# Routed tokens fetched by a slot-to-token table, and router products moved between the first up products

## The chip, the cores and the metric

The kernel runs on one core of a Trainium2 chip. The metric is the device time of one execution in microseconds (us).

## What is computed

Four stages follow each other on the residual `x` of 4 x 512 tokens by 512. The change lies in the second, a mixture of experts:

```python
sh_mid = gelu(einsum('th,ehd->ted', xt, Wsh_up), approximate=False)   # 2 shared experts, width 256
shared_out = einsum('ted,edh->th', sh_mid, Wsh_down)
probs = softmax(xt @ W_router, axis=-1)                               # 16 routed experts
top_v, top_i = top_k(probs, 2)
rt_mid = gelu(einsum('th,ehd->ted', xt, Wrt_up), approximate=False)
routed_out = einsum('ted,edh->th', rt_mid * gate[:, :, None], Wrt_down)
x = x + shared_out + routed_out                                       # xt: x after a layer norm
```

## The kernel before, in words

Each stage is a function with one instruction stream per engine, written out by hand; counting semaphores order the engines. Products are made in fp32r from three passes (`three_pass`, L47): high by high, high by low and low by high parts, where ScalarE makes the high part with a copy and VectorE the low part with a subtraction. `batch_product_phase` comes first, then `experts_phase` (L563), whose two parts the change touches, then `attention_phase` and `hadamard_ffn_phase`.

**Dense part.** VectorE writes the 16 normalised token tiles `xn` (128 tokens each; four make a batch). TensorE turns them over through seven PSUM banks (`turn_all`), ScalarE copies them out into `x32` (`evict`). `route(b)` multiplies the four tiles of batch b by the router weights, 16 columns wide, into PSUM bank 7. A unit s is one batch by one shared expert: `up(s)` is 24 products of 512 columns in two halves of 12, ScalarE's `unit(s)` makes the gelu and the high part, VectorE's `low(s)` the low part, `down(s)` is 24 products again in four tiles, and `add(s)` adds each tile to `x_res` in SBUF. The down tiles use three banks in turn, so the fourth waits for the add of the first. `turn_again(2)` and `turn_again(3)` turn batches 2 and 3 over again, because `x32` shares its memory with the operands of the dense part (`xT_hi`, `xT_lo`, `mid_hi`, `mid_lo`); they use the down banks, and their fourth tile waits for the first low part (`again_lo`).

**Routing.** VectorE runs `softmax_head`, `choose` (the two best experts of each token), `assign_places`, two `assign_slots` and `assign_tiles`; TensorE's `place_tokens` counts tokens in front of each one. Tokens are sorted by expert into 47 slot tiles of 128 places; the result is the place of each token (`slot[0]`, `slot[1]`) and the expert of each slot tile. SyncE first clears a DRAM buffer of 47 x 128 rows (L685). When `slot[i]` is there, GpSimd scatters `xn` into it with 16 indirect DMAs for each i (L750), after the clearing. SyncE's `load(0)` waits for all 32 (`scattered`, L709) before it fetches the first slot tile.

**Routed part.** For each of the 47 slot tiles SyncE's `load` brings the up and down weights of its expert (512 KB each, a ring of four) and the tokens `xg` (256 KB, a ring of three, freed by `xg_turned`), and stores the result `y` of six tiles earlier (256 KB, a ring of three). TensorE turns `xg` over, multiplies, and ScalarE and VectorE split weights and operands.

Of the kernel before, what the change touches and what calls it, by code (L numbers as in the profile page):

```python
# [14 lines left out]
P = 128  # L15
# [547 lines left out]
def experts_phase(nc, Wsh_up, Wsh_down, Wrt_up, Wrt_down, W_router, x_res, ident, stats, head_weights,  # L563
# [7 lines left out]
    xg_dram = nc.dram_tensor("tokens_by_expert", (NSLOT * P, D), F32, kind="Internal").ap()  # L571
    with ExitStack() as ctx:  # L572
# [8 lines left out]
        zeros = al.sb("zeros", [KD])  # L581
# [19 lines left out]
        tile_expert = al.sb("tile_expert", [NSLOT], I32)  # L601
        xn = al.sb("xn", [NT, D])
# [5 lines left out]
        turn_bank = bank[0:7]  # L608
        logits_bank = aux[:, 0:NT * E_RT].rearrange("p (t e) -> p t e", e=E_RT)
# [6 lines left out]
        x32 = [places[:, i] for i in (4, 5, 3, 1)]  # L616
# [32 lines left out]
        zeros_ready = al.sem("zeros_ready")  # L649
        cleared = al.sem("cleared")  # L650
# [4 lines left out]
        scattered = al.sem("scattered")  # L655
# [23 lines left out]
        def _(sp):  # L679
            sp.dma_start(router_raw[:, :, :], rows(W_router)).then_inc(router_in, 16)  # L680
            for i in range(E_SH):
                sp.dma_start(up_raw[:, i], rows(Wsh_up[i])).then_inc(up_in[i], 16)
                sp.dma_start(down_raw[:, i], rows(Wsh_down[i])).then_inc(down_in[i], 16)
            sp.wait_ge(zeros_ready, 2)
            sp.dma_start(xg_dram.rearrange("(t p) d -> p t d", p=P),  # L685
                         xg[:, 0:1, :].to_broadcast([P, NSLOT, D])).then_inc(cleared, 16)
# [4 lines left out]
            def load(i):  # L691
# [35 lines left out]
        def _(pool):  # L727
            nc.clear_and_free_semaphores(retired)
            pool.memset(zeros[:, :], 0.0).then_inc(zeros_ready, 1)
            pool.memset(xg[:, 0, :], 0.0).then_inc(zeros_ready, 1)  # L730
            pool.wait_ge(zeros_ready, 1)
# [8 lines left out]
            pool.wait_ge(const_ready, E_RT + 5)  # L740
# [139 lines left out]
        def _(dve):  # L880
# [35 lines left out]
            def choose():  # L916
# [4 lines left out]
                dve.wait_ge(const_ready, E_RT + 6)  # L921
# [32 lines left out]

            def norm(b):
# [93 lines left out]
        def _(pe):  # L1049
            def turn_all(b):  # L1050
# [30 lines left out]
            def up(s):  # L1081
                b, e = s // 2, s % 2
                if b == 0:
                    pe.wait_ge(up_ready, e + 1)
                pe.wait_ge(*((xT_ready, b + 1) if b < 2 else (again_ready, TB * (b - 1))))
                for k in range(KE):
                    if s >= 2:
# [3 lines left out]
                               lambda c: xT_hi[:, b % 2, c, :], lambda c: xT_lo[:, b % 2, c, :], KD).then_inc(up_done, 1)  # L1091

# [1060 lines left out]
```

## Time and profile before

| | us |
|---|---|
| median of 3 runs | 2151.6 (2144.74 to 2157.84) |
| the profiled execution, its time | 2148.4 |
| the profiled execution, its span on the core | 2146.8 |
| experts stage: first instruction to first weights of the next stage | 135.4 to 492.1 |

The profiled execution is 3.2 us below the median. Clock figures of TensorE are shares of 2.4 GHz as granted; 0.5 is 1.2 GHz.

### The profile page before, as it was taken

To read this page: it belongs to the slowest core of one execution; us is meant where nothing else is said; L and a number is where in the kernel's file an instruction comes from. 1 tells how busy PE (TensorE), PEld (TensorE's weight loads), DVE (VectorE), ACT (ScalarE), POOL (GpSimd) and SP (SyncE) were. 2 spreads that over 40 slices of the span, in tenths; PEclk is the share of its full clock that TensorE was granted. 3 is DMA by queue.
4 is the path that set the end of the run, shared out by engine and by line. 5 is a ranking of instruction groups with operands and counts; after the bars stand their busy time and mean duration, and the time that the engine had idled before them with its cause. 6 is when DMAs were issued, how large, how long until landed. Compare 5 with 4: busy or idle time off the path is not lost. (4 is left out here: it accounts for less than half of the span.)

```text
span 2146.8 us, 29048 instructions
## 1 busy us (share of the span) xinstructions
PE 2007.4 (94%) x9845; PEld 1663.7 (77%) x9849; DVE 1318.8 (61%) x2072; ACT 842.2 (39%) x1639; POOL 863.7 (40%) x739
## 2 busy tenths in 40 slices
PE   4987799994899999999999999999989999999999
PEld 4776577773778888888788888888867888888887
DVE  8975368887677766768676566666675333333333
ACT  4532158882434444445444444444432111111111
POOL 1104100003677766666766657665551222202200
PEclk9988899997999999999999999999999999999999
DMA  8366259994566656566555555555530011001002
GB/s 287 121 235 257 74 187 388 394 352 149 177 187 187 181 170 186 164 187 182 167 152 159 166 156 156 154 161 165 158 113 30 30 30 30 20 10 29 0 1 78
DMA packets 170320, 323.70 MB, mean 151 GB/s; under 512 B 16113, under 2 KB 41585, under 8 KB 170225
## 3 DMA queue, kind: packets, MB, share of 16 engines
q1 hardware_dynamic: 155120, 272.12, 40.8%
q0 software_dynamic: 15104, 50.34, 7.2%
q8 instruction: 55, 0.90, 0.2%
q14 instruction: 41, 0.33, 0.0%
HBM read 210.73 MB, written 111.67 MB: 150 GB/s over the span
## 5 line engine op out<-in xcount | busy, mean ns | idle before, releaser
L1393 POOL TENSOR_TENSOR t_pT_lo<-t_pT_raw,t_pT_hi 128x512 fp32r<-128x512 f32 x256 | 328.3, 1302 | 215.2 <-ACT t_pT_hi L1509 213.5
L1617 DVE TENSOR_REDUCE t_sums<-t_score 128x1 f32<-128x512 f32 x256 | 169.5, 688 | 130.3 <-PE t_score L52 129.9
L1991 DVE TENSOR_TENSOR f_lin<-f_lin,f_silu 128x512 f32<-128x512 f32 x64 | 44.8, 700 | 290.6 <-PE f_lin L52 290.6
L1524 ACT ACTIVATE t_probs<-t_score,t_sums 128x512 f32<-128x512 f32 x256 | 175.0, 684 | 84.3 <-DVE t_sums L1617 69.0
L1607 DVE STREAM_TRANSPOSE t_blocks<-t_probs 128x512 f32<-128x512 f32 x256 | 172.6, 693 | 20.4 <-ACT t_probs L1524 20.1
L1599 DVE SCALAR_TENSOR_TENSOR x_res<-t_out,t_sums,x_res 128x512 f32<-128x512 f32 x256 | 179.4, 741 | 4.7 <-PE t_out L52 4.5
L1509 ACT ACTIVATE t_pT_hi<-t_pT_raw 128x512 fp32r<-128x512 f32 x256 | 159.9, 625 | 1.1 <-DMA t_pT_raw<-turned_blocks 1.1
L1952 ACT ACTIVATE f_silu<-f_gate 128x512 f32<-128x512 f32 x64 | 38.3, 598 | 299.1 <-PE f_gate L52 299.1
L1503 ACT ACTIVATE t_o_hi<-t_o 128x512 fp32r<-128x512 f32 x64 | 38.3, 598 | 218.0 <-PE t_o L52 218.0
L1489 ACT ACTIVATE t_k_hi<-t_score 128x512 fp32r<-128x512 f32 x64 | 38.3, 598 | 204.6 <-PE t_score L52 200.9
L52 PE MATMUL t_score<-t_wv_hi,t_cT_hi 128*128 128x256 f32 x416 | 117.9, 283 | 0.7 <-ACT t_probs L1524 0.7
L52 PE MATMUL t_score<-t_wv_lo,t_cT_hi 128*128 128x256 f32 x416 | 117.9, 283 | 0.0
L52 PE MATMUL t_score<-t_wv_hi,t_cT_lo 128*128 128x256 f32 x416 | 117.8, 283 | 0.0
L52 PE MATMUL t_out<-t_wo_hi,t_o_hi 128*128 128x512 f32 x256 | 105.0, 410 | 12.8 <-DVE t_o_lo L1592 8.1
L2012 DVE TENSOR_TENSOR x_res<-f_down,x_res 128x512 f32<-128x512 f32 x128 | 88.1, 689 | 44.1 <-PE f_down L52 44.1
L52 PE MATMUL t_score<-t_k_hi,t_q_hi 128*128 128x512 f32 x256 | 102.8, 402 | 12.8 <-DVE t_v_lo L1586 4.8
L1582 DVE TENSOR_TENSOR t_k_lo<-t_score,t_k_hi 128x512 fp32r<-128x512 f32 x64 | 44.3, 691 | 113.2 <-ACT t_k_hi L1489 109.2
L52 PE MATMUL t_score<-t_cT_hi,t_wk_hi 128*128 128x512 f32 x256 | 101.5, 397 | 12.2 <-DVE t_cT_lo L1681 12.2
L1455 POOL DMA_INDIRECT t_blocks<-outputs_by_expert,slot x4 | 4.6, 1143 | 268.9 <-POOLq L572 267.9
L52 PE MATMUL t_q<-t_xT_hi,t_wq_hi 128*128 128x512 f32 x256 | 100.5, 393 | 2.8 <-DVE t_xT_lo L234 2.8
L52 PE MATMUL t_score<-t_k_lo,t_q_hi 128*128 128x512 f32 x256 | 101.3, 396 | 0.0
L52 PE MATMUL t_out<-t_wo_lo,t_o_hi 128*128 128x512 f32 x256 | 101.3, 396 | 0.0
(325 smaller groups left out, 6004.3 us busy)
## 6 DMA issues: line engine op xcount, KB each, us to landing
turned_blocks<-t_blocks SPq DMA_DIRECT2D x256, 256.0 KB
t_pT_raw<-turned_blocks SPq DMA_DIRECT2D x256, 256.0 KB, 4.1
e_up_raw<-in_L_ffn_Wrt_up_dram SPq DMA_DIRECT2D x47, 512.0 KB, 6.4
e_down_raw<-in_L_ffn_Wrt_down_dram SPq DMA_DIRECT2D x47, 512.0 KB, 5.9
tokens_by_expert<-e_xg SPq DMA_DIRECT2D x1, 12032.0 KB, 41.4
e_xg<-tokens_by_expert SPq DMA_DIRECT2D x47, 256.0 KB, 6.1
outputs_by_expert<-e_y_out SPq DMA_DIRECT2D x47, 256.0 KB, 6.2
wq_raw<-in_L_xattn_Wq_dram POOLq DMA_DIRECT2D x32, 256.0 KB, 4.6
```

The lines of the kernel that those rows point to most:

```text
L52: ins = pe.matmul(out, w(k), x(k), start=(k == 0 and j == 0), stop=(k == k_tiles - 1 and j == 2))
L1393: pool.tensor_tensor(pT_lo[:, q], pT_raw[:, q], f32(pT_hi[:, q]), ALU.subtract).then_inc(p_ready, 1)
L1489: act.activation(k_hi[:, :], score_bank[0][:, :], ACT.Copy).then_inc(k_hi_ready, 1)
L1503: act.activation(o_hi[:, :].rearrange("p (u q j) -> p q u j", q=Q4, j=BLK), o_bank[:, :].rearrange("p (q u j) -> p q u j", q=Q4, j=BLK), A ...
L1509: act.activation(pT_hi[:, q], pT_raw[:, q], ACT.Copy).then_inc(p_hi_ready, 1)
L1524: act.activation(probs[:, t % 2, :], score_bank[t][:, :], ACT.Exp, bias=neg_max[:, t:t + 1], accum_out=inv[:, p, t:t + 1]).then_inc(exp_re ...
L1582: dve.tensor_tensor(k_lo[:, :], score_bank[0][:, :], f32(k_hi[:, :]), ALU.subtract).then_inc(k_ready, 1)
L1599: dve.scalar_tensor_tensor(out=x_tile, in0=out_bank[t % 2][:, :], scalar=inv[:, p, t:t + 1], in1=x_tile, op0=ALU.mult, op1=ALU.add).then_i ...
L1607: dve.transpose(blocks[:, :, :, t, :].rearrange("p a t j -> p t a j"), probs[:, t % 2, :].rearrange("p (t a j) -> p t a j", a=Q4, j=BLK)). ...
L1617: dve.tensor_reduce(neg_max[:, t:t + 1], score_bank[t][:, :], AX.X, ALU.max, negate=True).then_inc(max_ready, 1)
L1991: dve.tensor_tensor(lin_bank[k][:, :], lin_bank[k][:, :], silu[:, k, :], ALU.mult).then_inc(mid_done, 1)
L2012: dve.tensor_tensor(x_tile, down_bank[t][:, :], x_tile, ALU.add).then_inc(added, 1)
```

## The change

It has two parts.

1. The 12032 KB clearing DMA and the 32 scatters go. SyncE stores `xn` in plain token order, 1 MB after each batch. The table runs the other way: VectorE's `mark(i)` makes, from `slot[i]`, one-hot rows of the place within a slot tile (`at_place`, 16 x 128) and one-hot rows of the slot tile times the token's row and tile number (`at_tile`, 16 x 2 x 47). TensorE's `find_tokens(i)` multiplies them, 16 products of 94 columns for each i, and `number_tokens` puts the sums together into `token`, the token of each slot. GpSimd then issues 47 gathers, one for each slot tile, straight into `xg`; from the fourth on each waits for `xg_turned`. SyncE no longer loads `xg`. Empty places have token 0.
2. All 16 tiles are turned over first. The router products stand between halves of `up(0)` and `up(1)`. Four other orders follow: ScalarE runs `unit(0)` before the second half of the split and before the exponential, `place_tokens` comes after `up(2)`, VectorE adds unit 0 before `choose`, and `low(2)` stands before `assign_places`. Three `x32` batches change places in memory, and `mid_hi` of unit 0 waits for `route(0)`.

```diff
-            sp.dma_start(xg_dram.rearrange("(t p) d -> p t d", p=P),
-                         xg[:, 0:1, :].to_broadcast([P, NSLOT, D])).then_inc(cleared, 16)
+            for b in range(B):
+                sp.wait_ge(xn_ready, TB * (b + 1))
+                sp.dma_start(xn_dram[b * S:(b + 1) * S, :].rearrange("(t p) d -> p t d", p=P),
+                             xn[:, TB * b:TB * (b + 1), :]).then_inc(xn_stored, 16)
...
-                if i >= XG_RING:
-                    sp.wait_ge(xg_turned, i - XG_RING + 1)
-                if i == 0:
-                    sp.wait_ge(scattered, 16 * 2 * NT)
-                sp.dma_start(xg[:, i % XG_RING, :], xg_dram[i * P:(i + 1) * P, :]).then_inc(xg_in[i % XG_RING], 16)
...
-            pool.wait_ge(cleared, 16)
-            for i in range(2):
-                pool.wait_ge(slots_ready, i + 1)
-                for j in range(NT):
-                    pool.indirect_dma_start(
-                        xg_dram[:, :], bass.IndirectOffsetOnAxis(ap=slot[i][:, j:j + 1], axis=0), xn[:, j, :], None,
-                        bounds_check=NSLOT * P - 1, oob_is_err=False).then_inc(scattered, 16)
+            pool.wait_ge(xn_stored, 16 * B)
+            pool.wait_ge(tokens_ready, 1)
+            for n in range(NSLOT):
+                if n >= XG_RING:
+                    pool.wait_ge(xg_turned, n - XG_RING + 1)
+                pool.indirect_dma_start(
+                    xg[:, n % XG_RING, :], None, xn_dram[:, :], bass.IndirectOffsetOnAxis(ap=token[:, n:n + 1], axis=0),
+                    bounds_check=NT * P - 1, oob_is_err=False).then_inc(xg_in[n % XG_RING], 16)
...
+                    if s == 0 and k == 0:
+                        act.wait_ge(routed, TB)
...
             shared_down_hi(0)
+            unit(0)
             hi(1)
-            shared_down_hi(1)
             act.wait_ge(shifted, 1)
             act.activation(probs[:, :, :], probs[:, :, :], ACT.Exp).then_inc(exp_ready, 1)
-            unit(0)
+            shared_down_hi(1)
...
+            def mark(i):
+                if i == 1:
+                    dve.wait_ge(token_found, 1)
+                link(dve.tensor_scalar(place_u[:, :], slot[i][:, :], P - 1, None, ALU.bitwise_and))
+                link(dve.tensor_scalar(tile_u[:, :], slot[i][:, :], 7, None, ALU.logical_shift_right))
+                link(dve.tensor_copy(place_of[:, :], place_u[:, :]))
+                link(dve.tensor_copy(tile_of[:, :], tile_u[:, :]))
...
+                link(dve.tensor_tensor(at_place[:, :, :], each(place_no[:, :], P), of(place_of[:, :], P), ALU.is_equal))
+                link(dve.tensor_tensor(at_tile[:, :, 0, :], each(tile_no[:, :], NSLOT), of(tile_of[:, :], NSLOT),
+                                       ALU.is_equal))
+                link(dve.tensor_tensor(at_tile[:, :, 1, :], at_tile[:, :, 0, :], of(tile_count[:, :], NSLOT), ALU.mult))
+                dve.tensor_scalar(at_tile[:, :, 0, :], at_tile[:, :, 0, :], row_no[:, 0:1], None,
+                                  ALU.mult).then_inc(marked, 1)
...
-            softmax_head()
             shared_up_lo(1)
             shared_down_lo(0)
+            dve.wait_ge(routed, 3 * TB)
+            low(0)
+            softmax_head()
             lo(1)
             shared_down_lo(1)
+            add(0)
             choose()
-            low(0)
             low(1)
+            low(2)
             assign_places()
             assign_slots(0, first)
-            add(0)
             assign_slots(1, rest)
             assign_tiles()
-            low(2)
             again_lo(2)
+            mark(0)
             add(1)
             low(3)
+            mark(1)
             add(2)
+            number_tokens()
             again_lo(3)
...
+            def find_tokens(i):
+                pe.wait_ge(marked, i + 1)
+                for j in range(NT):
+                    ins = pe.matmul(token_bank, at_place[:, j, :], at_tile[:, j, :, :].rearrange("p a n -> p (a n)"),
+                                    start=(i == 0 and j == 0), stop=(i == 1 and j == NT - 1))
+                ins.then_inc(token_found, 1)
...
             turn_all(0)
             turn_all(1)
-            route(0)
             turn_all(2)
+            turn_all(3)
+            up(0, between=lambda: route(0))
             route(1)
-            turn_all(3)
-            route(2)
+            up(1, between=lambda: route(2))
             route(3)
-            up(0)
-            up(1)
-            place_tokens()
             down(0)
             up(2)
+            place_tokens()
             turn_again(2)
             up(3)
             pe.wait_ge(again_ready, TB)
             down(1)
+            find_tokens(0)
             down(2)
+            find_tokens(1)
             turn_again(3)
```

The order of TensorE's instructions before, at the start of the experts stage (`e_bank` is PSUM; the products with `e_router_raw` are `route`, those from `ident` are `turn_all`):

```order
L1057 MATMUL e_bank<-ident,e_xn 128x128 x32
L1067 MATMUL e_bank<-e_router_raw,e_x 128x16 x16
L1057 MATMUL e_bank<-ident,e_xn 128x128 x16
L1067 MATMUL e_bank<-e_router_raw,e_x 128x16 x16
L1057 MATMUL e_bank<-ident,e_xn 128x128 x16
L1067 MATMUL e_bank<-e_router_raw,e_x 128x16 x32
L52 MATMUL e_bank<-e_xT_hi,e_up_hi 128x512
```

The same engine after the change, at the end of the first half of `up(0)`, with bank numbers:

```order
L52 MATMUL e_bank0<-e_xT_hi,e_up_hi 128x512
L52 MATMUL e_bank0<-e_xT_lo,e_up_hi 128x512
L52 MATMUL e_bank0<-e_xT_hi,e_up_lo 128x512
L1111 MATMUL e_bank7<-e_router_raw,e_x32 128x16 x16
L52 MATMUL e_bank1<-e_xT_hi,e_up_hi 128x512
```

A group of 16 router products now follows each half of 12 up products.

VectorE after the change, from the end of `assign_tiles` to `low(3)`, with `mark(0)` in it:

```order
L962 TENSOR_SCALAR e_tile_expert<-e_tile_f 1x47
L1001 TENSOR_TENSOR e_xT_lo<-e_bank,e_xT_hi 128x4x128 x4
L969 TENSOR_SCALAR e_place_u<-slot 128x16
L970 TENSOR_SCALAR e_tile_u<-slot 128x16
L971 CAST e_place_of<-e_place_u 128x16
L972 CAST e_tile_of<-e_tile_u 128x16
L975 TENSOR_TENSOR e_at_place<-e_place_no,e_place_of 128x2048
L976 TENSOR_TENSOR e_at_tile<-e_tile_no,e_tile_of 128x16x47
L978 TENSOR_TENSOR e_at_tile<-e_at_tile,e_tile_count 128x16x47
L979 TENSOR_SCALAR e_at_tile<-e_at_tile,e_row_no 128x16x47
L912 TENSOR_TENSOR x_res<-e_bank,x_res 128x512 x4
L904 TENSOR_TENSOR e_mid_lo<-e_bank,e_mid_hi 128x512 x2
```

The eight rows L969 to L979 are new and stand between `again_lo(2)` and `add(1)`; they come once more after `low(3)`.

## Rows read from the trace of the kernel before

**Rows 1.** Waits from 130 to 310 us: engine, tile, line, releaser: us, times, longest.
```profile
ACT e_bank L759 <- remote: 22.6, 1, 22.6
```
**Rows 2.** ScalarE's timeline in the hole: start, us, instruction, [idle before].
```profile
206.27 0.60 ACT L783 ACTIVATE e_xT_hi<-e_bank 128x512 fp32r<-128x512 f32 x1 [5.75 <-remote]
229.46 0.58 ACT L759 ACTIVATE e_bank<-e_bank 128x512 f32<-128x512 f32 x1 [22.59 <-remote]
```
**Rows 3.** GpSimd's timeline: the first and the last of the 32 scatters.
```profile
184.05 1.11 POOL L750 DMA_INDIRECT tokens_by_expert<-e_xn,slot  x1 [43.28 <-DVE slot L945]
...
223.94 0.98 POOL L750 DMA_INDIRECT tokens_by_expert<-e_xn,slot  x1 [0.30 <-issue]
```
**Rows 4.** Busy time by stretch: bounds, length, PE, PEld, DVE, ACT, POOL, PEclk, DMA share, GB/s.
```profile
147.20:151.00 3.80, 3.80 (x37) 3.80 (x36) 2.65 (x2) 0.92 (x2) 0.00 (x0) 1.00 1.04 409
154.00:164.20 10.20, 10.20 (x64) 10.20 (x64) 0.00 (x0) 2.45 (x3) 0.00 (x0) 0.67 1.05 408
164.20:168.20 4.00, 4.00 (x11) 3.13 (x11) 3.85 (x5) 3.87 (x4) 0.00 (x0) 0.51 1.05 409
207.00:229.00 22.00, 9.09 (x18) 5.24 (x18) 0.59 (x1) 0.00 (x0) 13.66 (x14) 0.58 0.48 191
380.00:420.00 40.00, 37.85 (x243) 31.35 (x241) 35.10 (x42) 35.39 (x61) 0.00 (x0) 1.00 1.06 394
```
**Rows 5.** TensorE's timeline, dense part: routers, end of place_tokens, first of up(4), first of down(3).
```profile
141.89 3.64 PE L1067 MATMUL e_bank<-e_router_raw,e_x 128*128 128x16 f32 x32
...
153.72 10.56 PE L1067 MATMUL e_bank<-e_router_raw,e_x 128*128 128x16 f32 x64
...
177.56 1.12 PE L1111 MATMUL e_bank<-e_chosen,e_ones 128*128 128x256 bf16 x16
...
243.70 0.48 PE L52 MATMUL e_bank<-e_xT_hi,e_up_hi 128*128 128x512 f32 x1
...
249.38 0.40 PE L52 MATMUL e_bank<-e_down_hi,e_mid_hi 128*128 128x512 f32 x1
```
**Rows 6.** VectorE's timeline: lo(0), choose from its first step, routing steps.
```profile
146.44 2.28 DVE L962 TENSOR_TENSOR e_xT_lo<-e_x,e_xT_hi 128x2048 fp32r<-128x2048 f32 x1
...
170.72 0.41 DVE L918 TENSOR_REDUCE e_top<-e_probs 128x16 f32<-128x256 f32 x1
...
177.29 2.48 DVE L894 TENSOR_TENSOR e_mid_lo<-e_bank,e_mid_hi 128x512 fp32r<-128x512 f32 x4
179.69 0.17 DVE L930 TENSOR_SCALAR e_tiles_u<-e_bank 128x16 uint32<-128x16 f32 x1
...
182.93 0.17 DVE L945 CAST slot<-e_slot_f 128x16 uint32<-128x16 f32 x1
...
187.29 0.93 DVE L949 TENSOR_TENSOR e_passed<-e_tile_no,e_run 1x752 f32<-1x752 f32 x1
...
189.22 0.17 DVE L952 TENSOR_SCALAR e_tile_expert<-e_tile_f 1x47 int32<-1x47 f32 x1
```
**Rows 7.** ScalarE's timeline: first shared_up_hi, evict(2), hi(1), the load of gelu's table.
```profile
144.07 1.08 ACT L787 ACTIVATE e_up_hi<-e_up_raw 128x1024 fp32r<-128x1024 f32 x1
...
146.06 2.06 ACT L769 ACTIVATE e_x<-e_bank 128x512 f32<-128x512 f32 x4 [0.91 <-PE e_bank L1057]
...
164.32 1.91 ACT L777 ACTIVATE e_xT_hi<-e_x 128x2048 fp32r<-128x2048 f32 x1 [7.87 <-PE e_bank L1067]
...
167.50 1.28 ACT L759 ACT_TABLE_LOAD   x1
```
**Rows 8.** ScalarE's timeline in the routed part: two store waits in a row.
```profile
473.77 0.60 ACT L861 ACTIVATE e_y_out<-e_bank 128x512 f32<-128x512 f32 x1 [0.41 <-DMA outputs_by_expert<-e_y_out]
...
477.71 0.60 ACT L861 ACTIVATE e_y_out<-e_bank 128x512 f32<-128x512 f32 x1 [0.41 <-DMA outputs_by_expert<-e_y_out]
```
**Rows 9.** ScalarE's timeline while 16 gathers of the attention stage are issued.
```profile
510.45 0.60 ACT L1498 ACTIVATE t_v_hi<-t_score 128x512 fp32r<-128x512 f32 x1 [4.44 <-remote]
```
**Rows 10.** TensorE's timeline there: the last product that the row of rows 9 waits for.
```profile
508.32 0.28 PE L52 MATMUL t_score<-t_wv_hi,t_cT_lo 128*128 128x256 f32 x1
```

More of the change, by code:

```diff
@@ L564, in experts_phase @@
                   y_dram, gate, slot, retired):
-    xg_dram = nc.dram_tensor("tokens_by_expert", (NSLOT * P, D), F32, kind="Internal").ap()
+    xn_dram = nc.dram_tensor("normalised_tokens", (NT * P, D), F32, kind="Internal").ap()
     with ExitStack() as ctx:
@@ L580, in experts_phase @@
         router_raw = al.sb("router_raw", [KD, E_RT])
-        zeros = al.sb("zeros", [KD])
         probs = al.sb("probs", [NT, E_RT])
@@ L601, in experts_phase @@
         tile_expert = al.sb("tile_expert", [NSLOT], I32)
+        place_no, row_no, tile_count = al.sb("place_no", [P]), al.sb("row_no", [1]), al.sb("tile_count", [NT])
+        place_u, tile_u = al.sb("place_u", [NT], U32), al.sb("tile_u", [NT], U32)
+        place_of, tile_of = al.sb("place_of", [NT]), al.sb("tile_of", [NT])
+        at_place = al.sb("at_place", [NT, P], BF16)
+        at_tile = al.sb("at_tile", [NT, 2, NSLOT], BF16)
+        token = al.sb("token", [NSLOT], U32)
         xn = al.sb("xn", [NT, D])
@@ L608, in experts_phase @@
         turn_bank = bank[0:7]
+        token_bank = aux[:, (NT + 1) * E_RT:(NT + 1) * E_RT + 2 * NSLOT]
         logits_bank = aux[:, 0:NT * E_RT].rearrange("p (t e) -> p t e", e=E_RT)
@@ L615, in experts_phase @@
         places = Alloc(nc, routing, "e").sb("x32", [6, KD, S])
-        x32 = [places[:, i] for i in (4, 5, 3, 1)]
+        x32 = [places[:, i] for i in (4, 3, 5, 1)]
         routing.close()
@@ L648, in experts_phase @@
         const_ready = al.sem("const_ready")
-        zeros_ready = al.sem("zeros_ready")
-        cleared = al.sem("cleared")
+        xn_stored = al.sem("xn_stored")
+        marked, token_found, tokens_ready = al.sem("marked"), al.sem("token_found"), al.sem("tokens_ready")
         chosen_ready = al.sem("chosen_ready")
@@ L654, in experts_phase @@
         map_ready = al.sem("map_ready")
-        scattered = al.sem("scattered")
         up_done = al.sem("up_done")
@@ L728, in _ @@
             nc.clear_and_free_semaphores(retired)
-            pool.memset(zeros[:, :], 0.0).then_inc(zeros_ready, 1)
-            pool.memset(xg[:, 0, :], 0.0).then_inc(zeros_ready, 1)
-            pool.wait_ge(zeros_ready, 1)
             for e in range(E_RT):
@@ L739, in _ @@
                       allow_small_or_imprecise_dtypes=True).then_inc(const_ready, 1)
-            pool.wait_ge(const_ready, E_RT + 5)
+            pool.iota(place_no[:, :], [[1, P]], base=0, channel_multiplier=0,
+                      allow_small_or_imprecise_dtypes=True).then_inc(const_ready, 1)
+            pool.iota(row_no[:, :], [[1, 1]], base=0, channel_multiplier=1,
+                      allow_small_or_imprecise_dtypes=True).then_inc(const_ready, 1)
+            pool.iota(tile_count[:, :], [[1, NT]], base=0, channel_multiplier=0,
+                      allow_small_or_imprecise_dtypes=True).then_inc(const_ready, 1)
+            pool.wait_ge(const_ready, E_RT + 8)
             pool.affine_select(below[:, :], ones[:, :], [[1, P]], ALU.is_gt, 0.0, base=0,
@@ L920, in choose @@
                 link(dve.tensor_tensor(probs[:, :, :], probs[:, :, :], wide(inv), ALU.mult))
-                dve.wait_ge(const_ready, E_RT + 6)
+                dve.wait_ge(const_ready, E_RT + 9)
                 pick(probs[:, :, :], first[:, :, :], gate[0])
@@ L953, in assign_tiles, with number_tokens @@
                                   ALU.min).then_inc(map_ready, 1)
+            def mark(i):
[5 more added lines that the diff above has]
+                link(dve.tensor_copy(tile_of[:, :], tile_u[:, :]))
+                each = lambda a, n: a.unsqueeze(1).to_broadcast([P, NT, n])
+                of = lambda a, n: a.unsqueeze(2).to_broadcast([P, NT, n])
+                link(dve.tensor_tensor(at_place[:, :, :], each(place_no[:, :], P), of(place_of[:, :], P), ALU.is_equal))
[4 more added lines that the diff above has]
+                                  ALU.mult).then_inc(marked, 1)
+            def number_tokens():
+                dve.wait_ge(token_found, 2)
+                link(dve.tensor_copy(tile_f[:, :], token_bank[:, 0:NSLOT]))
+                dve.scalar_tensor_tensor(out=token[:, :], in0=token_bank[:, NSLOT:2 * NSLOT], scalar=float(P),
+                                         in1=tile_f[:, :], op0=ALU.mult, op1=ALU.add).then_inc(tokens_ready, 1)
             def norm(b):
@@ L1079, in turn_again, with up @@
                     ins.then_inc(again_turned, 1)
-            def up(s):
+            def up(s, between=None):
                 b, e = s // 2, s % 2
                 if b == 0:
+                    pe.wait_ge(x32_ready, NT - 5 if s else NT)
                     pe.wait_ge(up_ready, e + 1)
@@ L1091, in up @@
                                lambda c: xT_hi[:, b % 2, c, :], lambda c: xT_lo[:, b % 2, c, :], KD).then_inc(up_done, 1)
+                    if between and k == 0:
+                        between()
             def down(s):
@@ L1170, in turn_mid @@
                 if n == 0:
-                    pe.wait_ge(slots_ready, 2)
+                    pe.wait_ge(tokens_ready, 1)
                 elif n == 1:
```

1 line of the change is left out of this document (removed).

## The prediction

> **What bounds the kernel now.** I read three views, in this order. First the busy time by stretch, to find where TensorE is not at work in the experts stage: between 207 and 229 us it is busy for 9.09 of 22 us at clock 0.58, with the DMA engines at a share of 0.48 [rows 4]. Then the waits, to see who is late: ScalarE stood still for 22.6 us in front of one gelu, with a releaser that the trace only calls "remote" [rows 1]. Its timeline shows two such waits after one another, 5.75 and 22.59 us [rows 2]. Last GpSimd's timeline: the first of 32 scatters is issued at 184.05, the last at 223.94 [rows 3]. The hole starts some 10 us after the first and ends some 4 us after the last. The data bandwidth does not explain it (share 0.48, while other stretches run at 1.04 to 1.06 with TensorE busy [rows 4]). So the engines lack something else while scatters flow. I take it to be their instructions, which the page of the profile lists as DMA queues of their own; that is argued, not shown.
>
> After the dense part the routed part is bound by DMA: share 1.06 and 394 GB/s from 380 to 420 us [rows 4]. A slot tile takes 473.77 to 477.71 = 3.94 us, of which ScalarE waits 0.41 us for a store of three tiles earlier [rows 8]. A slot tile moves 512 + 512 + 256 + 256 KB = 1.57 MB, and 1.57 MB in 3.94 us is 399 GB/s, the stretch's rate within 2%.
>
> **The dense part, step by step.** Before, `up(4)` starts at 243.70 us [rows 5], and nothing disturbs TensorE from there to the routed part, before or after the change: nine blocks of 24 products at 249.38 - 243.70 = 5.7 us [rows 5]. So the gain of this part is how much earlier `up(4)` starts. I take it in two steps.
>
> Start of `up(0)`. ScalarE ends the first weight split at 144.07 + 1.08 = 145.2 and then has 8 tiles to evict, at 2.06 / 4 = 0.51 each [rows 7]: 149.3. VectorE has xT_lo at 146.44 + 2.28 = 148.7 [rows 6]. So `up(0)` can start at about 149.5. Then follow four halves of 2.8 us (half of 5.7, less the block's share of waits) and four router groups of 3.64 us [rows 5], together 25.8 us at full clock. The clock is the open term. In the old order it was 1.00 while routers ran until 151 us and 0.67 from 154 to 164.2, where 64 router instructions took 10.56 us instead of 2 x 3.64 = 7.3 [rows 4, 5]; after it the first 4.0 us of `up(0)` ran at 0.51 [rows 4]. Lower bound: no low clock, 0. Upper bound: all of it low, four halves at about 5.1 and four groups at 5.3, which adds 15.8. TensorE idles for two microseconds ahead of `up(0)`, so I expect one low start, +2, and, as one of three old router groups was followed by a fall, about one more, +2. The last router group ends at T = 149.5 + 25.8 + 4 = 179.3 us.
>
> From T to `up(4)`, where VectorE sets the pace:
> - `softmax_head` 0.9 and `hi(1)` 1.9 beside it [rows 7], `lo(1)` 2.3 [rows 6], the second down split 1.2: T + 5.5. `down(0)` has begun at T, but its fourth tile needs the first add. Adds end at T + 8.3.
> - `choose`, 170.72 to 177.29, 6.6 us, and four low parts 2.5 [rows 6]: T + 17.4. ScalarE loads two more tables (exponential, gelu again) at 1.28 each [rows 7]; exp is ready near T + 3.6 and the gelus near T + 8, both hidden under VectorE's adds. Were that cover gone, they would cost 2.6.
> - `assign_places` and the first slots 179.69 to 183.10, 3.4; the second slots 1.1; `assign_tiles` 187.29 to 189.39, 2.1 [rows 6]: T + 24.0. The first `again_lo` 0.7: T + 24.7. TensorE has finished `up(2)`, `place_tokens` (16 products in 1.12 us, rows 5 have them) and three tiles of `turn_again(2)` by T + 18.3 and now waits some 6.5 us. The old order hid this under `down(0)` and `up(2)`. I add 2 us for the clock after this gap.
> - Fourth tile 0.5, `up(3)` 5.6 + 2, `down(1)` 5.6: T + 38.4. Behind it stands `find_tokens(0)`, 16 short products like those of `place_tokens`, 1.2: T + 39.6. `mark(0)` ran on VectorE beside `up(3)` and costs nothing there.
> - `mark(1)` waits for that. Its price: four small steps at about 0.2, 2048 elements at 2.3 as in `lo(0)`, and three of 752 elements at 0.93 at most (`e_passed` has 752) [rows 6], together 5.9. VectorE gets to `add(2)` at T + 46.2, and `down(2)`, whose fourth tile needs it, ends at T + 48.3 instead of T + 45.2. `find_tokens(1)` 1.2, `number_tokens` 0.6, then `turn_again(3)` behind it: `up(4)` at T + 52.
>
> 179.3 + 52 = 231.3, and 243.7 - 231.3 = 12.4 us earlier. The hole itself was larger than that. What takes the rest is the longer chain on VectorE.
>
> **The rest of the change.** The 32 scatters and the clearing go, also from SyncE's way to `load(0)`; the four stores of `xn`, 4 MB, take 10 us at 409 GB/s [rows 4], beside the first turns, and `up(0)` needs only the shared weights queued ahead of them. Cost nothing; if the weights came late, at most a few us. The first three gathers are issued near 230 us, some 45 us before their use. The tokens move the same 256 KB per tile, so I leave the 3.94 us alone. GpSimd issues a gather in about 1 us as it did a scatter [rows 3] and has 3.94. Three tiles ahead are 11.8 us, and an xg load is not late by then.
>
> The price of gathers on the other engines is the least known term. While 16 gathers of the attention stage were issued, one ScalarE instruction came at 510.45 though the last product that it needed began at 508.32 and took 0.28 [rows 9, 10]: 1.85 us late, again "remote". That is the near bound: most such lateness hides in the rings, I count one, 1.8 us. The far bound is the scatter hole: about 34 us for 32 scatters (from 164 us on, 16 blocks of 5.7 and some 6 us of turns and counting would end at 261; the dense part ends at 243.7 + 9 x 5.7 = 295 [rows 5]), 1.06 us each, times 44 gathers = 47 us. I take the near one because it is the same operation. Below nothing: if the own queue of the gathers helps, the 0.41 us wait goes, 47 x 0.41 = 19 us.
>
> Sum against the profiled execution: 2148.4 - 12.4 + 1.8 = **2137.8 us, say 2138**. The profiled execution lies 3.2 us below the median of the runs, so this is 13.6 us below that median.
>
> The Trainium skill ("DMA: Bandwidth & Descriptors", section "Queues, rings and completion order") says that each DMA engine takes turns between its queues at packet granularity. By that rule an instruction load would be held up by a few packets, never for 22 us; the rows of the hole speak against the rule, or against instructions as the cause. By the rule alone the 1.8 us would be nothing, 2136. The same page (section "Issuing engines are not separate DMA queues") says that transfers from all engines run on the same 16 DMA engines, which speaks against a gain from the own queue of the gathers.
>
> **The rivals.**
> - *Gathers starve the engines in the routed part as scatters did.* Place: any of TensorE, ScalarE or VectorE between 275 and 470 us, with "remote" or "issue" waits. Price up to 47 us: 2138 + 47 = 2185. It decides from 0.3 us per gather on (13 us, the whole gain). For it: GpSimd's transfers would be nearly always in flight there, at saturated DMA. Against it: rows 9 and 10. Slower.
> - *The dense gain is given back.* The clock falls after each router group (T up to 15.8 - 4 = 12 us later), or the hole was not caused by the scatters and comes again. Then only some 2 to 5 us stay: about 2146. For it: the router groups are as long as before; TensorE now has three new waits (after `down(0)`'s third tile, in `turn_again(2)`, in `down(2)`). No change within the measurement.
> - *The routed part speeds up.* SyncE is rid of `xg_turned` and ScalarE's 0.41 us goes: 2138 - 19 = 2119. Against it: the DMA share of 1.06 [rows 4] is already full. Faster.
>
> **How the numbers follow.** Over or under 0.5% (10.8 us) is what a measurement of this kernel can tell from no change. Forecast 0.50, starvation 0.13, given back 0.23, routed part faster 0.12, other 0.02. The forecast lies 13.6 us below the median, only 3 beyond the bound, so a quarter of it falls within: faster 0.38 + 0.12 = 0.50; same 0.12 + 0.18 = 0.30; slower 0.13 + 0.05 + 0.02 = 0.20. The range takes in the best clock and some of the faster routed part at the lower end, 2138 - 4 - 12 = 2122, and at the upper end the dense gain lost and a third of the starvation, 2148 + 15 = 2163; what is left out are the far ends of two rivals.
>
> **What would show it.** Right: `up(4)` near 231 us with no "remote" wait over 3 us before it; a wait of 5 to 8 us in front of the fourth tile of `turn_again(2)`; a clock of 0.5 in part of 149 to 179 us; a routed period of 3.9 to 4.0 us. Wrong: a routed period above 4.2 with waits called remote or issue (starvation), one below 3.8 (own queue helps), `up(4)` after 240 us (given back), or VectorE's `mark` far from 5.9 us.

## The result and the profile after

The change made the kernel 0.53% faster: 2142.55 us median (2135.65 to 2147.45, 16 runs) against 2154.57 us (2144.27 to 2160.96, 16 runs), ratio 0.9947 with a 95% interval of 0.9934 to 0.996, or 12.0 us. The forecast was 2138 us (2122 to 2163), 13.6 us below the median then known.

The profiled execution after took 2147.45 us (span 2145.8), the longest of its 16 runs, and 5 us above their median; the one before (2148.4) was 6 us below its median of 16. This pair of profiles is therefore only 1 us apart, and the 12 us can't be read off it alone. The mechanisms can, and later profiles add the rest.

ScalarE's waits of the changed kernel from 130 to 310 us (engine, tile, line, releaser: us, times, longest). Nothing in this view is called remote, and none of them is 22 us long for one instruction in the middle of the dense part, as in [rows 1]:

```profile
ACT e_bank L767 <- PE e_bank L52: 43.1, 13, 7.2
ACT e_xT_hi L793 <- PE e_bank L1121: 22.0, 4, 12.0
ACT e_xT_hi L787 <- PE e_bank L1111: 20.1, 1, 20.1
ACT e_x L779 <- PE e_bank L1101: 11.2, 4, 10.2
```

Busy time by stretch after (columns as in [rows 4]). The first row holds most of the routers between up products: 25 us at a mean clock of 0.66. In the second, the stretch of the old hole, 207 to 229 us, TensorE is busy for 18.99 us instead of 9.09, at 0.84 instead of 0.58. The last is the routed part, 386 GB/s where [rows 4] has 394:

```profile
155.00:180.00 25.00, 25.00 (x119) 21.96 (x119) 1.29 (x2) 1.78 (x3) 0.00 (x0) 0.66 0.14 53
207.00:229.00 22.00, 18.99 (x86) 15.03 (x86) 16.44 (x26) 2.86 (x5) 0.00 (x0) 0.84 0.28 95
380.00:420.00 40.00, 38.14 (x236) 31.23 (x236) 33.78 (x40) 34.46 (x59) 12.96 (x10) 1.00 1.05 386
```

TensorE's timeline after (start, us, instruction, [idle before]); its places answer to [rows 5]. `up(0)` starts at 150.71; the first router group stands 2.8 us behind it; then the first products of `place_tokens`, the fourth tile of `turn_again(2)`, `up(3)`, `down(1)`, `find_tokens(0)`, the fourth tile of `down(2)`, `find_tokens(1)`, `turn_again(3)` and `up(4)`:

```profile
150.71 0.47 PE L52 MATMUL e_bank<-e_xT_hi,e_up_hi 128*128 128x512 f32 x1 [2.73 <-DVE e_up_lo L1006]
...
153.55 4.27 PE L1111 MATMUL e_bank<-e_router_raw,e_x 128*128 128x16 f32 x32
...
199.98 0.29 PE L1156 MATMUL e_bank<-e_chosen,e_below 128*128 128x272 bf16 x1 [1.84 <-DVE e_chosen L936]
...
209.56 1.12 PE L1121 MATMUL e_bank<-ident,e_xn 128*128 128x128 f32 x4 [6.97 <-DVE e_xT_lo L1001]
210.33 0.78 PE L52 MATMUL e_bank<-e_xT_hi,e_up_hi 128*128 128x512 f32 x1
...
217.81 0.39 PE L52 MATMUL e_bank<-e_down_hi,e_mid_hi 128*128 128x512 f32 x1
...
223.41 0.87 PE L1090 MATMUL e_bank<-e_at_tile,e_at_place 128*128 128x94 bf16 x16
...
232.21 0.80 PE L52 MATMUL e_bank<-e_down_hi,e_mid_hi 128*128 128x512 f32 x1 [3.65 <-DVE x_res L912]
...
234.94 1.48 PE L1090 MATMUL e_bank<-e_at_tile,e_at_place 128*128 128x94 bf16 x16
236.21 3.22 PE L1121 MATMUL e_bank<-ident,e_xn 128*128 128x128 f32 x16
239.19 0.48 PE L52 MATMUL e_bank<-e_xT_hi,e_up_hi 128*128 128x512 f32 x1
```

VectorE's timeline after: `mark(0)`. It takes 211.95 to 217.49, 5.5 us, and `mark(1)` the same from 226.03:

```profile
211.95 0.16 DVE L969 TENSOR_SCALAR e_place_u<-slot 128x16 uint32<-128x16 uint32 x1
...
212.78 2.29 DVE L975 TENSOR_TENSOR e_at_place<-e_place_no,e_place_of 128x2048 bf16<-128x2048 f32 x1
215.11 0.95 DVE L976 TENSOR_TENSOR e_at_tile<-e_tile_no,e_tile_of 128x752 bf16<-128x752 f32 x1
216.09 0.94 DVE L978 TENSOR_TENSOR e_at_tile<-e_at_tile,e_tile_count 128x752 bf16<-128x752 bf16 x1
217.07 0.42 DVE L979 TENSOR_SCALAR e_at_tile<-e_at_tile,e_row_no 128x752 bf16<-128x752 bf16 x1
```

The turns of `xg` on TensorE bound the routed part (a line's own view: duration min, median, max, then first and last start). Before, then after:

```profile
L1153 PE MATMUL e_bank<-ident,e_xg x188: 270/273/331, 294.2 to 477.4; 128*128 128x128 f32 x188
```

```profile
L1200 PE MATMUL e_bank<-ident,e_xg x188: 270/272/273, 289.5 to 476.3; 128*128 128x128 f32 x188
```

So the profiled pair shows 4.7 us gained up to the first turn, and 3.6 us given back in the routed part: 186.8 instead of 183.2 us.

### The profile page after: what moved, and what is told of

Its sections match the earlier page's. It is cut to its first block and busy times, and to the rows that moved or that the text cites. A ratio compares the mean times of both kernels' runs of the same rounds, so it can differ in the third digit from the quotient of the medians.

```text
span 2145.8 us, 29120 instructions
## 1 busy us (share of the span) xinstructions
PE 2016.8 (94%) x9877; PEld 1670.4 (78%) x9881; DVE 1329.1 (62%) x2090; ACT 843.7 (39%) x1641; POOL 890.1 (41%) x755
## 5 line engine op out<-in xcount | busy, mean ns | idle before, releaser
L757 POOL DMA_INDIRECT e_xg<-normalised_tokens,e_token x47 | 59.2, 1259 | 263.1 <-PE e_bank L1200 166.4
L52 PE MATMUL t_out<-t_wo_hi,t_o_lo 128*128 128x512 f32 x256 | 102.5, 400 | 0.0
```

The costliest lines, as they stand in the source:

```text
L52: ins = pe.matmul(out, w(k), x(k), start=(k == 0 and j == 0), stop=(k == k_tiles - 1 and j == 2))
L757: pool.indirect_dma_start(xg[:, n % XG_RING, :], None, xn_dram[:, :], bass.IndirectOffsetOnAxis(ap=token[:, n:n + 1], axis=0), bounds_chec ...
```

## The experiments

Twelve runs follow, in three jobs, each job on one chip of its own and beside the kernel before. The kernel before itself was not the same on all of them: 2154.25 us on one, as in the first result, and 2125.42 and 2125.99 us on the other two. I call the first sort **H** (the first result fits it too) and the other sort **N**. Chip and job can't be told apart here, since each of the three jobs had its own chip and that of the first result is not on record: "a chip of sort H" may as well be a condition of that job. A second look at the kernel before on N has no hole, though its 32 scatters are issued at the same pace.

The first job, on a chip of sort N, ran the changed kernel, its two parts alone, and the old kernel without scatters.

**after_again**: the changed kernel, no edit. 

> The changed kernel once more, for a second profile. My theory: the medians differ by 12 us because the hole of the old kernel costs more in most executions than in the profiled one, so the gap here is again 9 to 14 us with up(4) near 239 us. Rival, the profiled execution of the changed kernel was an odd one (its time, 2147.45, is the slowest of 16): then this profile shows up(4) below 235 or a routed part shorter by 3 us or more.

Measured: 2139.63 us (6 runs) against 2125.42, ratio 1.0074 (1.0045 to 1.0103). The sign is turned over, so the theory fell, and the rival's sign is there: `up(4)` starts at 233.77, below 235. The changed kernel takes what it took on H to within 3 us; the kernel before is 29 us faster than there.

**table_only**: the table and the gathers, with the old dense order.

```diff
             turn_all(0)
             turn_all(1)
+            route(0)
             turn_all(2)
+            route(1)
             turn_all(3)
-            up(0, between=lambda: route(0))
-            route(1)
-            up(1, between=lambda: route(2))
+            route(2)
             route(3)
+            up(0)
+            up(1)
+            place_tokens()
             down(0)
             up(2)
-            place_tokens()
```

(And the same for ScalarE and VectorE, with `mark(0)` still behind `again_lo(2)`, `mark(1)` behind `low(3)`.) 

> The table and the gathers with the old order of routers, up products, gelus and adds. My theory that the scatters make the hole: 8 to 16 us faster than the kernel before, as fast as the whole change or faster, because up(0) starts late but the chain on VectorE is hidden as before. Rival, the new order of the dense part carries the gain: then within 3 us of the kernel before.

Measured: 2130.3 us (12 runs), ratio 1.0041 (1.002 to 1.0062). It is slower, not 8 to 16 us faster: there was no hole to take away.

**order_only**: the new dense order, with the old scatters and loads. 

> The new order of the dense part with the old clearing and scatters. My theory: no gain or slower by up to 8 us, because the scatters come later, still stop the engines for over 20 us, and the chain on VectorE is exposed. Rival, the order carries the gain: faster by 6 us or more.

Measured: 2132.75 us (12 runs), ratio 1.0042 (1.0025 to 1.0059). That is within the "slower by up to 8 us" of the theory, but not for its reason, since the scatters stop nothing here. By the medians the parts cost 4.9 and 7.3 us where there is no hole, and together 14.2; by the recorded ratios, which are not the quotients of the medians, it is 0.4% each (9 us) and 0.7% together (16 us).

**no_scatter**: the kernel before without its scatters; `load(0)` waits for the clearing alone.

```diff
-                    pool.indirect_dma_start(
-                        xg_dram[:, :], bass.IndirectOffsetOnAxis(ap=slot[i][:, j:j + 1], axis=0), xn[:, j, :], None,
-                        bounds_check=NSLOT * P - 1, oob_is_err=False).then_inc(scattered, 16)
```

> The kernel before without its 32 scatters: the routed part computes on the cleared rows, so its routed outputs are left out. My theory: the hole goes, up(4) starts near 215 us instead of 243.7 and the time falls by 25 to 34 us. Rival, the hole has another cause (clearing, place of an instruction load): less than 8 us.

Measured: 2128.07 us (10 runs), ratio 1.0022 (1.0003 to 1.0041). On N the scatters cost nothing, so the theory of 25 to 34 us fell there. What that says of H was open until the last job.

The second job, on the other chip of sort N.

**before_again**: the kernel before, no edit. 

> The kernel before once more, for its profile beside the others of this job. Theory now: the 22.6 us hole belongs to the chip of the first measurement, where instruction supply suffers under scatters; here up(4) starts at 220 to 228 us without a remote wait. Rival: the hole is here too and the times differ elsewhere.

Measured: 2125.16 us (8 runs), ratio 0.9991 (0.9961 to 1.0021). `up(4)` starts at 223.13 without a remote wait, as the theory had it. The stretch of the hole (columns as in [rows 4]), and GpSimd's waits in the dense part:

```profile
207.00:229.00 22.00, 20.62 (x96) 16.44 (x96) 9.99 (x15) 5.04 (x9) 16.82 (x18) 1.00 0.53 214
```

```profile
POOL tokens_by_expert L750 <- issue: 9.5, 31, 0.3
```

GpSimd issues scatters for 16.82 of these 22 us, more than in [rows 4] (13.66), at a higher DMA share (0.53), and TensorE is busy for 20.62 us. The same instructions do no harm on this chip.

**direct_xg**: the changed kernel with SyncE's plain 256 KB loads of `xn_dram` in place of the gathers, whose loop on GpSimd goes (routed outputs left out).

```diff
+                sp.dma_start(xg[:, i % XG_RING, :], xn_dram[m * P:(m + 1) * P, :]).then_inc(xg_in[i % XG_RING], 16)
```

> The changed kernel with SyncE loading a plain tile of the stored tokens in place of each gather; routed outputs are left out. Theory: the gathers cost the routed part 4 to 7 us (first to last turn of xg 187 to 190 us with them, 183 without), so this is 4 to 7 us faster than the changed kernel. Rival, the stores of xn or the order make it longer: no difference.

Measured: 2140.38 us (5 runs), ratio 1.0071 (1.0043 to 1.0099). The time is that of the gathers, so the rival held and the 4 to 7 us did not come. Its stores land in 6.4 us instead of 7.0, and its routed part is 185.9 us (table below), so the gathers are not what makes most of the routed part longer.

**swap**: the changed kernel with `up(3)` ahead of `turn_again(2)`, against the 6.97 us wait.

```diff
-            turn_again(2)
             up(3)
+            turn_again(2)
```

> The changed kernel with up(3) ahead of turn_again(2), so that it lies beside the routing chain on VectorE. Theory: the 7 us wait before the fourth tile goes, 5 to 7 us faster than the changed kernel. Rival, the wait moves to down(1), whose operands come later: under 2 us.

Measured: 2136.3 us (9 runs), ratio 1.0052 (1.0034 to 1.0069), 3.3 us below after_again, on another chip of the same sort. The wait leaves three smaller ones in its place (1.41, 1.41 and 1.58 us), so some 4 of the 7 us are won (100.8 instead of 104.8 in the table below), less than the 5 to 7 expected.

**swap_late**: swap, with both marks behind `add(3)` and `add(4)`, and both `find_tokens` behind `up(5)` and `up(6)`. 

> As swap, and both mark steps and the token products moved to after add(3) and add(4), where each unit leaves VectorE about 7 us. Theory: also the 3.65 us wait in down(2) and one of 1 to 2 us for the clock go, 9 to 13 us faster than the changed kernel and faster than the kernel before where that has its hole, even with it where it has none. Rival, the marks delay adds there: no better than swap.

Measured: 2137.66 us (8 runs), ratio 1.006 (1.004 to 1.008). The dense part ends 4.3 us earlier than in swap (first turn at 277.0 instead of 281.3), but the routed part is 3.5 us longer. The median is no better than that of swap: the rival held, and the 9 to 13 us did not come.

The third job landed on a chip of sort H.

**after_b**: the changed kernel, no edit. 

> The changed kernel once more, on whatever chip this lands on. If the sign of the change depends on the chip: where the kernel before shows no remote hole (median near 2125), ratio 1.005 to 1.009, up(4) about 12 us later than in the kernel before of that chip; where the kernel before shows the hole (median near 2150), ratio 0.993 to 0.997. If instead the ratio is a matter of single runs and not of the chip, it comes out within 1.000 +- 0.003 here.

Measured: 2141.59 us (8 runs) against 2154.25 (12 runs), ratio 0.9947 (0.9924 to 0.997). The first result repeats, as expected for a kernel before that shows the hole. The sign of this change goes with the chip or the job, not with single runs.

**no_scatter_b**: as no_scatter. 

> The kernel before without its 32 scatters (the slot buffer stays cleared, so the routed outputs are left out). On a chip without the hole: 2126 to 2130, as before within 0.2%, since the scatters then cost nothing. On a chip with the hole: scatters as its cause give about 34 us less than the kernel before (2116 to 2122 against 2150); a hole that has another cause stays, with a remote wait of ScalarE over 10 us in front of a gelu between 200 and 240 us, and the time stays within 5 us of the kernel before.

Measured: 2127.93 us (4 runs), ratio 0.9882 (0.9847 to 0.9917), that is 26.3 us less. It fell between the two expectations in size, but the kind is clear: with no scatters there is no hole, and the median is that of no_scatter on N (2128.07) to 0.2 us, with only four runs here. In this job the old kernel takes 2154.25, without scatters 2127.93, and the changed one 2141.59: 26.3 us are won with the scatters, and the rest of the change gives 13.7 back. The stretch of the hole:

```profile
207.00:229.00 22.00, 20.62 (x97) 16.56 (x96) 9.51 (x15) 5.62 (x10) 0.00 (x0) 1.00 0.00 1
```

**gather_there**: 32 gathers from the slot buffer into four spare tiles, in the scatters' place, each from the fifth on after the one four before it has landed (routed outputs left out).

```diff
-                        xg_dram[:, :], bass.IndirectOffsetOnAxis(ap=slot[i][:, j:j + 1], axis=0), xn[:, j, :], None,
+                        spare[:, n % 4, :], None, xg_dram[:, :], bass.IndirectOffsetOnAxis(ap=slot[i][:, j:j + 1], axis=0),
```

> The kernel before with 32 gathers from the slot buffer into four spare SBUF tiles in the place of the 32 scatters (routed outputs left out). Theory that any indirect DMA in this place is harmless on a chip without the hole: no wait called remote over 3 us between 180 and 260 us, first turn of xg within 3 us of the kernel before. Theory that a scatter differs from a gather by its writes to DRAM: same here, and on a chip with the hole no hole in this kernel.

Measured: 2142.16 us, one run, 14.2 us above no_scatter_b. The theory that only a scatter does it, by its writes to DRAM, fell: gathers do it too, if less. The other theory was about a chip without the hole and stays untested, since this one has it. ScalarE's timeline in `turn_again(3)`, with two waits for something that is no engine, while GpSimd issues a gather every 1.3 us (in before_again the same four copies come between 221.35 and 224.0):

```profile
235.63 0.60 ACT L788 ACTIVATE e_xT_hi<-e_bank 128x512 fp32r<-128x512 f32 x1 [6.34 <-issue]
239.84 1.08 ACT L788 ACTIVATE e_xT_hi<-e_bank 128x512 fp32r<-128x512 f32 x2 [3.61 <-remote]
```

and VectorE's, two of the waits on it:

```profile
225.13 0.69 DVE L907 TENSOR_TENSOR x_res<-e_bank,x_res 128x512 f32<-128x512 f32 x1 [4.26 <-remote]
...
236.26 0.69 DVE L973 TENSOR_TENSOR e_xT_lo<-e_bank,e_xT_hi 128x512 fp32r<-128x512 f32 x1 [6.25 <-issue]
```

**table_late**: table_only with both marks moved behind `add(3)` and `add(4)`, `find_tokens` behind `up(5)` and `up(6)`.

```diff
             down(1)
-            find_tokens(0)
             down(2)
-            find_tokens(1)
...
             up(5)
+            find_tokens(0)
             down(4)
             up(6)
+            find_tokens(1)
```

> Table without the new dense order, and both mark steps moved behind the adds of units 3 and 4, find_tokens behind up(5) and up(6). Theory: the table's two marks cost nothing there, so the dense part ends 2 to 5 us earlier than table_only's (first turn of xg near 265 instead of 268.7), while the routed part keeps its 187 to 189 us: 2126 to 2130, 2 us either side of the kernel before on a chip without the hole, 15 to 25 us below it on one with. Rival, the gathers set the pace of what follows and the routed part gives the dense gain back: 2130 to 2133.

Measured: 2124.81 us (5 runs, 2121.33 to 2137.31), ratio 0.9886 (0.9846 to 0.9926) to the kernel before, and 16.8 us below after_b in the same job. It is faster than both kernels on H, and 29.4 us below the kernel before, more than the 15 to 25 expected; its five runs spread over 16 us. It is not clear of no_scatter_b (2127.93). Its two `find_tokens` cost TensorE 0.7 us each and waits of 0.65 and 0.73 us in front of them, and the fourth tile of `down(2)` no longer waits. The first turn comes at 267.5, not at the 265 expected, and the routed part takes 186.0 us, 1 less than expected. It was not run on N, and table_only not on H, so what the late marks alone are worth was not measured.

**The profiles side by side.** T is the end of the last router group. The four stretches add up to the span.

| kernel | sort | T | T to first turn of `xg` | first to last turn | rest |
|---|---|---|---|---|---|
| before | H | 164.3 | 129.9 | 183.2 | 1669.4 |
| no_scatter_b | H | 163.5 | 100.4 | 185.2 | 1670.4 |
| gather_there | H | 173.3 | 115.6 | 183.1 | 1668.6 |
| table_late | H | 164.0 | 103.5 | 186.0 | 1669.7 |
| after | H | 184.4 | 105.1 | 186.8 | 1669.5 |
| after_b | H | 179.4 | 104.6 | 189.3 | 1670.4 |
| before_again | N | 172.9 | 100.7 | 181.9 | 1667.1 |
| no_scatter | N | 174.9 | 101.0 | 186.2 | 1670.0 |
| table_only | N | 163.6 | 105.1 | 187.6 | 1669.8 |
| order_only | N | 179.8 | 98.0 | 182.7 | 1669.8 |
| after_again | N | 179.3 | 104.8 | 190.1 | 1663.1 |
| direct_xg | N | 180.2 | 104.8 | 185.9 | 1669.8 |
| swap | N | 180.5 | 100.8 | 185.3 | 1667.2 |
| swap_late | N | 181.5 | 95.5 | 188.8 | 1669.1 |

The column from T to the first turn holds the hole: 129.9 with scatters on H, 100.4 without them, 100.7 with them on N. That is 29.5 us for 32 scatters, 0.92 us each, and 15.2 us or 0.47 us each for gathers in their place. The rest after the last turn varies by 7.3 us, without a pattern by sort; differences of a few us between two profiles can come from there.

## Why the prediction was right

- **The hole and its cause.** It held that the hole of 34 us in [rows 1 to 3] comes from the scatters. Shown: taking them away takes the hole away (29.5 us in the profiles, 26.3 in the medians). From rows alone the size was 34, since I let the dense part without a hole end at 261; it ends at 263.9.
- **What is missing while scatters flow** stays open, but the trace of before says two things that I had not read. TensorE also stands between products of one tile of `down(1)`, where its program has no wait for a semaphore (`three_pass`, L47). The five such pauses from 219 to 228 us alone are 6.9 us. So late semaphores are not all of it:

```profile
218.23 0.58 PE L52 MATMUL e_bank<-e_down_hi,e_mid_hi 128*128 128x512 f32 x1 [2.42 <-issue]
219.63 0.58 PE L52 MATMUL e_bank<-e_down_lo,e_mid_hi 128*128 128x512 f32 x1 [0.82 <-issue]
222.43 0.59 PE L52 MATMUL e_bank<-e_down_hi,e_mid_lo 128*128 128x512 f32 x1 [2.21 <-issue]
225.22 0.59 PE L52 MATMUL e_bank<-e_down_hi,e_mid_hi 128*128 128x512 f32 x1 [2.21 <-issue]
226.63 0.58 PE L52 MATMUL e_bank<-e_down_lo,e_mid_hi 128*128 128x512 f32 x1 [0.82 <-issue]
228.04 0.59 PE L52 MATMUL e_bank<-e_down_hi,e_mid_lo 128*128 128x512 f32 x1 [0.82 <-issue]
```

And the prediction's own guess, instructions held up in their DMA queues, is not what the profile shows. Its two instruction queues moved no packet between 187 and 244 us, and the next one came 0.6 to 1.4 us behind the start of `up(4)` (243.70), as in no_scatter_b, before_again, gather_there and order_only, where `up(4)` starts at 213.66, 223.13, 230.84 and 227.56. TensorE was out of the hole 14 us before that packet. A shortage that doesn't show in these queues is not ruled out.

- **Start of `up(0)` and T = 179.3.** Three profiles: 184.43, 179.41 and 179.30. The term that moved is the clock, for which I took +4 between 0 and 15.8. In the profiled execution it was about +8, since `up(0)` also began 1.2 us later than the 149.5 of the text (150.71). Four router groups took 4.27, 3.78, 4.58 and 3.93 us. In the other two the clock's part was about +4.5, and the sum came out as it was written; +4 was a choice within 15.8, so that it came out so close is partly luck.
- **From T to `up(4)`, 52 us.** Measured 54.8, 54.5 (after_b) and 54.5 (after_again). The wait in front of the fourth tile of `turn_again(2)` was forecast at some 6.5 us and is 6.97; `up(3)` at 5.6 + 2 and is 217.81 - 210.33 = 7.5; `mark` at 5.9 and is 5.5. The step that is short is the end: `down(2)`'s fourth tile came after a wait of 3.65 us and then ran at a low clock, as did `find_tokens(1)` (1.48 us instead of 0.87) and `turn_again(3)` (3.22). I had put the clock's price behind the first wait and none behind the second, which is most of the 2.8 us; the rest is `add(2)`, which came about 1 us later than written.
- **`up(4)` at 231.3.** It started at 239.19, 233.90 and 233.77. Its gain in the first pair is 4.5 us, not 12.4: 5.1 us of the shortfall are T, 2.8 the step behind it. With after_b, from another job, it is 243.70 - 233.90 = 9.8 us.
- **Gathers, 1.8 us.** The far bound, 47 us, is ruled out: the view of waits of the routed part holds no remote wait, and "issue" stands for 14.5 us on TensorE's weight loads in 37 pieces of at most 1.7. With gathers the routed part is 185.3 to 190.1 us (seven profiles); with plain loads and no scatters it is 185.2, 186.2 and 185.9. The means are 187.7 and 185.8, 1.9 apart, but the two groups overlap, and two of the three plain ones have the old order as well. The mechanism of the 1.8, one late instruction called remote, did not occur, so the closeness of the size is luck. Against the kernel before the routed part is 3.6 us (after) and 6.1 us (after_b) longer: this term of the sum was too small.
- **What the sum did not have.** Plain loads without scatters are themselves 2 to 4 us longer there than plain loads behind scatters or gathers (181.9 to 183.2). That is no price of the gathers, and I have no explanation: TensorE's waits for `xg` are gone after the change, yet the stretch is longer, at 386 instead of 394 GB/s. Why stays open.
- **ScalarE's store wait.** The wait of [rows 8] did not go as the third rival had it. It grew between 300 and 470 us from 22.1 us in 39 pieces to 25.7 in 38 (first row below; the second is the "issue" wait above). The 0.41 us was a small one: the mean before was 0.57. The stores land in 7.0 us instead of 6.2. The DMA was full, as the text said against that rival.

```profile
ACT e_y_out L871 <- DMA outputs_by_expert<-e_y_out: 25.7, 38, 2.0
...
PEld e_bank L52 <- issue: 14.5, 37, 1.7
```

- **The signs.** There is no remote wait before `up(4)`, the wait in `turn_again(2)` is 6.97 us, and the granted clock was 0.50 from 157.7 to 162.9 us, all as written. The period of a slot tile was not 3.9 to 4.0: 4.05 us (after), 4.11 (after_b) and 4.13 (after_again), against 3.98 before; it stays below the 4.2 of starvation.
- **Luck in the total.** The sum is 10.6 us below the profiled execution. The spans of the profiles differ by only 1.0 us (after) and 3.1 us (after_b), because the dense gain is 2.6 to 7.9 us smaller than 12.4 and the routed part 1.8 to 4.3 us longer than allowed. The 12.0 us between the medians came about because the profiled execution before lies 6.2 us below the median of its 16 runs, not 3.2, while those of after and after_b lie 4.9 and 3.7 us above theirs. The granted clock fits that: in the third job two runs of the kernel before took 2143.8 and 2144.1 us at a mean clock of 0.979, and three took 2156.1, 2156.8 and 2158.7 at 0.971. Which stretch loses the clock is not shown, since no run of the kernel before near its median was profiled on H; the late kind of router block in the last section, some 9 us, is a candidate.

The rule that DMA engines take turns between queues at packet granularity (the Trainium skill, "DMA: Bandwidth & Descriptors", section "Queues, rings and completion order") would have a held-up instruction load come through after a few packets. By that rule no hole of 22.6 us comes from a data queue. The runs on N agree with it (scatters cost nothing). Those on H do not refute it, since no instruction packet moved in the hole; of the two readings that the prediction left open, it is the one against instruction loads as the cause.

**What the prediction had no place for** is a second chip. It allowed that the hole might not be due to scatters, and a "given back" at 0.23; it did not allow that the kernel before is hole-free on another chip. There the same sum would have read: hole 0, so a loss. The part that carries over is the cost of the new order and the early marks. On H, without scatters in either, the change's dense part ends at 284.0 where the old order's ends at 263.9. By steps of TensorE, order_only (on N, where scatters do no harm) against no_scatter_b (on H): `down(0)` starts 1.8 us later, `up(2)` 3.3, its end with the wait for `choose` 5.2, `up(3)` 12.4, `down(1)` 13.9, and `up(4)` 13.9 (227.56 against 213.66). The marks where they stand add 6.3 us (after_b starts `up(4)` at 233.90). These steps say that the routing chain on VectorE, hidden behind other products in the old order, is exposed in the new one from `down(0)` on.

## What to carry to other kernels

A wait that the profile can only call remote, at a moderate DMA share and with a burst of indirect DMAs beside it, is worth one run without the burst, before anything else is re-ordered. Here that alone was worth 26 us on one sort of chip, and the rest of the change gave 14 of them back there and cost 14 on the other. Make the two edits apart. Moving `mark` to where VectorE has slack (behind `add(3)` and `add(4)` instead of ahead of `add(1)` and `add(2)`) made the dense part 4 us shorter from swap to swap_late, but not the kernel; only table_late, which drops the new order too, was faster than both kernels, and it ran on H alone. And before a gain of half a per cent is believed, run the kernel before on a second chip.

## What the hardware did that I had not expected

- **A hole that comes with the chip (or the job).** The same kernel takes 2154 us on one sort of chip and 2125 us on the other; without its scatters it takes 2128 on both. What differs between them is not known. The attention stage, which no kernel here changes, tells the sorts apart too: during or just after its bursts of gathers ScalarE shows a wait called remote of 3.6 to 6.1 us in each of the six profiles on H, and in none of the eight on N. First after_b and table_late (H), then before_again (N):

```profile
505.73 0.60 ACT L1545 ACTIVATE t_v_hi<-t_score 128x512 fp32r<-128x512 f32 x1 [5.70 <-remote]
```

```profile
486.02 0.60 ACT L1543 ACTIVATE t_v_hi<-t_score 128x512 fp32r<-128x512 f32 x1 [6.07 <-remote]
```

```profile
485.72 0.60 ACT L1498 ACTIVATE t_v_hi<-t_score 128x512 fp32r<-128x512 f32 x1 [2.28 <-PE t_score L52]
```

- **Back to back or spread.** On H, gathers issued every 1.3 us stalled the engines by 15 us in 32. Issued every 4.1 us, in the routed part, they left no remote wait. One run, with gathers from another buffer and beside other work, doesn't show that the pace is what matters.
- **Two outcomes of the old router block.** The old order ends its routers at 163.5 to 164.3 us in some profiles and at 172.9 to 174.9 in others, on both sorts of chip. TensorE is busy without a pause in both; the granted clock from 154 to 164 us is 0.65 to 0.67 in the one and 0.50 in the other. First no_scatter_b, then before_again:

```profile
154.00:164.00 10.00, 10.00 (x61) 9.90 (x61) 0.45 (x2) 2.12 (x3) 0.00 (x0) 0.66 1.05 408
```

```profile
154.00:164.00 10.00, 10.00 (x50) 10.00 (x49) 0.00 (x0) 4.28 (x6) 0.00 (x0) 0.50 1.05 410
```

These 9 us fit the spread of the runs of the kernel before (2110 to 2132 on N). That of the changed kernel is 2138 to 2141 in after_again, but with six runs only, and 2135.65 to 2147.45 in the 16 runs of the first result. The profile of before on which the prediction rests was of the early kind.
